# A one-core decoder layer: the step sizes' products in stacked float32r parts, the first normalisation on ScalarE, and orders planned anew

## The chip, the cores and the metric

One core of a Trainium2 chip runs one decoder layer in one launch. The metric is the device time in microseconds (us) of one execution, the median of several runs. A core has TensorE (matmuls, into PSUM), VectorE (DVE), ScalarE (ACT), GpSimd (POOL) and SyncE (SP), whose queue starts all DMAs here.

## The reference

The input x is 4 batches of 512 rows of 512. Three parts are each added to x; the layer norm before each has no gain and no bias.

```python
x = x + attn(layernorm(x), w_qkv, w_o)       # 16 heads of 32, rotary, causal softmax
x = x + ssm(ctx, z=layernorm(x), ...)        # selective scan, 16 states, 512 channels
x = x + ffn(layernorm(x), w_fc, w_proj)      # two ternary linears 512 -> 2048 -> 512, each with
                                             # its own layer norm, gelu between
# the scan's inputs, per batch (L = 512):
u = silu(conv4(in_proj_w @ ctx) + conv_b)                     # [512 channels, L]
x_dbl = x_proj_w @ u                                          # [48, L]: 16 step rows, 16 B, 16 C
delta = softplus(dt_proj_w @ x_dbl[:16] + dt_proj_b)          # the step sizes, [512, L]
state = state * exp(delta * A) + (delta * u) * B_t            # A = -exp(A_log), a recurrence over L
y = sum_n state_n * C_n + D * u;   y = y * silu(z)
```

The step-size product must keep float32 precision, since delta stands in an exponent.

## The kernel before

All activations of a batch stay in SBUF. Attention works on 32 slots (a pair of heads of one batch: `s` scores, `e` exponentials, `t` transposes, `pv` and `rz` output and row sums). The state space part has 16 states per batch; each state is two pieces of 128 partitions by two times 512 columns: ScalarE makes the factors (`exp`, L1502), GpSimd the inputs (`dbu`, L1382, with a row of B broadcast by DMA, ring of two), VectorE scans (L1911), TensorE transposes the result (`ht`, L1834), VectorE adds it times C into y (L1933). The last batch is scanned in two halves. The feed-forward part works on 16 tiles of 128 rows (`fc` L1881, `proj` L1891); it needs the tile's x after the state space part and can begin once attention is over. The ternary weights are made on the way (`wsum`, `tern`).

These parts are interleaved. The order of the work on each of the five engines is written out before the kernel by `plan()`: `follows(item)` lists for each item on which engines it runs, how long in the planner's view and what it needs; `schedule()` gives each item a due time out of tables of numbers (`WEIGHT`, `SLOT_AT`, `STATE_AT`, `FRONT`, `SSM_FRONT` and more), and `plan()` picks for each engine the ready item with the earliest due time. It also places the results in PSUM banks and sets how many filler transposes (L1708) TensorE does before an item. Each engine runs its list strictly in order, and waits on semaphores.

Around the change, per batch:

- First layer norm, 4 tiles of 128 rows, two buffers `x_in`. SP loads the tile; VectorE takes mean and variance (`ln1a`, L1940 to L1944); GpSimd takes the power -0.5 (L1435); VectorE normalises in place (`ln1b`, L1949); TensorE transposes (L1721); ScalarE copies into `xn_t` (L1543).
- Step sizes. TensorE projects u into 48 rows (`xproj`, L1739), ScalarE copies them into `x_dbl` (L1565), which frees the bank. SP stores the B rows to DRAM (L1272), from where they are broadcast. TensorE transposes the C rows (`ct`, L1748) and makes four products of [16 x 128] by [16 x 512] in float32 (`dt`, L1755). ScalarE makes four operations of each (L1583 to L1589), then VectorE (batch 0) or GpSimd (batches 1 to 3) puts `delta` together, and GpSimd multiplies by u (`du`, L1409).

`Own.done` and `Own.settle` are an engine's wait for its own earlier instructions.

Of the kernel before, what the change touches and what calls it, by code (L numbers as in the profile page):

```python
# [5 lines left out]
F32 = mybir.dt.float32  # L6
# [7 lines left out]
P = 128  # L14
# [23 lines left out]
CH = 256  # L38
HALF_L = L // 2
# [43 lines left out]
def scan_before(j):  # L83
# [25 lines left out]
WEIGHT = {'pe': {'ln1b': -40.55,  # L109
        'inproj': -66.23,  # L110
        'xproj': 52.84,
        'ct': 36.01,
        'dt': 36.18,
        'rot': -16.7,
        'v': 28.68,
        's': 10.49,
        't': 0.51,
        'pv': -14.56,
        'rz': -9.8,
        'wo': 20.24,  # L120
        'ht': -8.38,
        'gt': 52.57,
        'wtot': 64.6,
        'xt': 153.75,
        'fc': -34.46,
        'ht_ffn': 7.6,
        'proj': 117.47},
 'act': {'carry': -68.1,
         'exp': 22.09,
         'skip': -67.92,  # L130
         'ht': -65.82,
         'ln1b': 172.89,
# [36 lines left out]
         'ht_ffn': 69.64,
         'fc': -48.69,  # L170
         'hstat': 223.03,
         'hn': -111.41,
         'hq': 17.54,
         'proj': 159.09},
 'pool': {'delta': 72.43,
          'dbu': -26.46,
          'du': -36.26,
          'lo': 113.37,
          'xadd': -42.2,
          'ln1a': -84.79,  # L180
          'ln2a': 128.64,
          'xa': -39.22,
          'xc': -52.97,
          'hstat': -183.22,
          'rot': -14.91,
          'xt': 51.35,
          'ht_ffn': -79.49},
 'sp': {'xload': -185.09,
        'cload': -80.68,
        'wload': -88.67,  # L190
        'lo': -89.88,
        'xproj': -71.92,
        'bcload': 100.82,
        'stack': 114.14,
        'resid': 7.11,
        'x2store': 63.43,
        'fwload': -65.57,
        'fxload': -41.54,
        'proj': 96.57,
        'tstore': 61.26,  # L200
        'twload': -63.21,
        'xt': 86.28,
        'ht_ffn': -16.23}}

SLOT_AT = [-70.63, -1.1, -20.34, 0.54, 115.31, 113.43, 78.09, 84.3, 153.3, 152.56, 215.37, 144.34, 186.75, 225.59, 239.97,
 325.62, 293.69, 254.46, 305.8, 346.92, 332.64, 445.39, 439.93, 450.71, 470.36, 463.38, 493.97, 567.05, 578.9,
 568.09, 553.9, 607.86, 786.52]

STATE_AT = [[-17.64, -2.42, 62.4, 26.71, 61.61, 103.25, 162.05, 173.2, 146.17, 89.95, 152.03, 51.3, 193.65, 157.21, 168.06,
  150.72],  # L210
 [191.57, 187.06, 218.99, 260.04, 204.72, 261.35, 243.06, 286.61, 294.78, 379.55, 307.54, 422.57, 367.67, 396.65,
  396.57, 447.53],
 [446.31, 544.57, 382.08, 534.02, 388.94, 578.24, 382.41, 635.04, 607.17, 663.93, 751.89, 725.61, 755.13, 667.46,
  787.52, 1081.77],
 [752.3, 624.59, 697.07, 746.88, 725.98, 520.82, 754.79, 594.25, 720.37, 634.17, 682.62, 610.64, 746.41, 688.17,
  656.56, 687.14, 673.05, 780.99, 733.21, 805.86, 823.88, 779.55, 826.28, 843.2, 719.63, 839.02, 824.33, 637.9,
  921.74, 785.09, 853.63, 766.31]]
# [1982 lines left out]
```

## Time and profile before

| | |
|---|---|
| median of 3 runs | 970.09 us (966.22 to 970.52) |
| profiled execution | 970.87 us, span 969.1 us, mean granted TensorE clock 0.979 |
| TensorE busy | 893.0 us, 92%, 5426 instructions |
| VectorE busy | 854.3 us, 88%, 1167 |
| ScalarE busy | 735.0 us, 76%, 1476 |
| GpSimd busy | 615.8 us, 64%, 439 |
| DMA | 153.55 MB, mean 158 GB/s |

The span is from the first to the last instruction of the profiled execution; 1.8 us of its time lie around it. TensorE has two rows, PE for matmuls and PEld for weight loads, which overlap. A float32 matmul stands as two records; a float32r one as one record, although its type is printed as f32. Two neighbouring records overlap in time, so what an operation occupies is read from start to next start.

### The profile page before, as it was taken

The numbers are of one execution on the slowest core, as the hardware profiler recorded it, in microseconds if no ns is written. First come the engines' busy times: TensorE is split into PE (matmuls) and PEld (weight loads), VectorE is DVE, ScalarE is ACT, GpSimd is POOL, SyncE is SP. The second block draws the span as 40 slices with busy tenths as digits, with TensorE's granted clock in tenths as the row PEclk, the third lists the DMA queues.
The fourth block names the chain that finished last, engine by engine and source line by source line (L and its number), as shares of the span: only waits on it lengthen the run. The fifth ranks groups of instructions, "written<-read, shape, count | busy, mean of one in ns | idle before, by whom it ended". The sixth has DMA issues, their size and how long they took to land.

```text
span 969.1 us, 17249 instructions
## 1 busy us (share of the span) xinstructions
PE 893.0 (92%) x5426; PEld 573.7 (59%) x5426; DVE 854.3 (88%) x1167; ACT 735.0 (76%) x1476; POOL 615.8 (64%) x439
## 2 busy tenths in 40 slices
PE   7998779889999999989999999789889999999998
PEld 5464546556776656677656577567745455544544
DVE  4698999999999979899998989999989989998741
ACT  4988955935757996786988775896589999999551
POOL 0286954655347638993663989535679889878620
PEclk9999999799999999999999999799999999999999
DMA  6678849778847555274734645643147566755383
GB/s 211 234 225 267 224 124 230 197 206 216 225 144 205 165 182 148 72 210 112 185 101 136 206 132 183 220 110 111 38 72 179 112 135 129 151 106 125 62 166 77
DMA packets 146296, 153.55 MB, mean 158 GB/s; under 512 B 90448, under 2 KB 94800, under 8 KB 145952
## 3 DMA queue, kind: packets, MB, share of 16 engines
q1 hardware_dynamic: 146208, 152.45, 59.0%
q8 instruction: 46, 0.75, 0.3%
q14 instruction: 42, 0.34, 0.1%
HBM read 103.00 MB, written 28.44 MB: 136 GB/s over the span
## 4 chain that ended last, share of the span: by engine, by line
PE 45%; ACT 17%; DVE 15%; issue 11%; POOL 8%; DMA 3%; SPq 1%; ACTq 0%; POOLq 0%; DVEq 0%
PE ps L1765 7%; PE ps L1891 7%; PE ps L1834 6%; PE ps L1881 5%; DVE hb L1911 5%; ACT p_q L1615 4%; POOL hb L1382 4%; PE ps L1808 3%; ACT ps L1502 3%; PE ps L1778 3%; PE ps L1846 3%; DVE y_acc L1933 2%; ACT p_t L1631 2%; PE ps L1739 2%; DVE m_col L2008 2%
## 5 line engine op out<-in xcount | busy, mean ns | idle before, releaser
L1382 POOL TENSOR_TENSOR hb<-du,b_bc 128x1024 f32<-128x1024 f32 (+1 forms) x160 | 308.4, 1951 | 93.1 <-PE ps L1834 87.3
L1911 DVE TENSOR_TENSOR_SCAN hb<-ps,hb 128x1024 f32<-128x1024 f32 (+1 forms) x128 | 256.6, 2012 | 15.8 <-ACT ps L1502 12.2
L1502 ACT ACTIVATE ps<-delta,a_neg 128x511 f32<-128x511 f32 (+2 forms) x320 | 179.4, 598 | 86.2 <-DVE hb L1911 82.0
L1933 DVE SCALAR_TENSOR_TENSOR y_acc<-ps,ct,y_acc 128x512 f32<-128x512 f32 x256 | 178.6, 736 | 14.0 <-PE ps L1834 13.3
L1834 PE MATMUL ps<-ident,hb 128*128 128x128 f32 x1088 | 150.7, 281 | 24.8 <-DVE hb L1911 8.3
L1834 PEld LDWEIGHTS ps<-ident,hb 128*128 128x128 f32 x1088 | 124.0, 143 | 55.4 <-issue 16.5
L1615 ACT ACTIVATE p_q<-ps,m_col 128x512 f32<-128x512 f32 (+3 forms) x256 | 132.0, 538 | 10.5 <-DVE m_col L2008 9.5
L1765 PE MATMUL ps<-xn_t,w_ring 128*128 128x512 f32 x256 | 120.7, 616 | 1.0 <-ACT p_t L1631 0.5
L1881 PE MATMUL ps<-t_fc,xt 128*128 128x512 f16 x512 | 116.6, 379 | 1.8 <-ACT h_sb L1679 1.8
L1891 PE MATMUL ps<-t_pr,ht 128*128 128x512 f16 x512 | 113.0, 379 | 0.5 <-DMA ht<-hs 0.5
L1631 ACT ACTIVATE p_t<-ps 128x512 f32<-128x512 f32 x160 | 86.0, 612 | 26.8 <-PE ps L1808 26.6
L1808 PE MATMUL ps<-ident,p_q 128*128 128x128 f32 x640 | 88.0, 284 | 14.8 <-ACT p_q L1615 7.0
L1808 PEld LDWEIGHTS ps<-ident,p_q 128*128 128x128 f32 x640 | 73.0, 145 | 34.3 <-ACT p_q L1615 14.7
L2008 DVE TENSOR_REDUCE m_col<-ps 128x1 f32<-128x512 f32 (+2 forms) x192 | 86.3, 500 | 3.3 <-PE ps L1793 2.8
L1891 PEld LDWEIGHTS ps<-t_pr,ht 128*128 128x128 f16 x512 | 49.8, 98 | 60.2 <-issue 0.8
L1881 PEld LDWEIGHTS ps<-t_fc,xt 128*128 128x128 f16 x512 | 49.9, 98 | 55.0 <-ACT h_sb L1679 2.3
L1765 PEld LDWEIGHTS ps<-xn_t,w_ring 128*128 128x128 f32 x256 | 48.2, 198 | 53.7 <-issue 50.4
L1789 PE MATMUL ps<-k_st,q_st 128*128 128x512 f32 (+3 forms) x256 | 70.3, 377 | 7.8 <-DVE y_acc L1933 5.0
L1137 POOL TENSOR_TENSOR hs<-h_sb,hs 128x1024 f16<-128x1024 f32 x28 | 60.3, 2161 | 8.6 <-ACT hs L1669 8.6
L1416 POOL TENSOR_TENSOR hl<-hl 128x512 f32<-128x512 f32 x16 | 21.6, 1348 | 67.7 <-DVE hl L1996 67.7
L1778 PE MATMUL ps<-w_ring,xn_t 128*128 128x256 f32 x256 | 58.2, 381 | 2.5 <-DMA w_ring<-in_w_attn 2.2
L1846 PE MATMUL ps<-w_ring,o_t 128*128 128x256 f32 x256 | 57.4, 380 | 1.2 <-DVE xr L2031 1.0
(137 smaller groups left out, 1484.2 us busy)
## 6 DMA issues: line engine op xcount, KB each, us to landing
w_ring<-in_w_attn SPq DMA_DIRECT2D x32, 512.0 KB, 4.5
qk_d<-hl SPq DMA_DIRECT2D x64, 256.0 KB
q_st<-qk_d SPq DMA_DIRECT2D x64, 256.0 KB, 4.4
b_bc<-bc_d SPq DMA_DIRECT2D x48, 256.0 KB, 4.5
raw<-in_w_fc SPq DMA_DIRECT2D x16, 512.0 KB, 4.6
raw<-in_w_pr SPq DMA_DIRECT2D x16, 512.0 KB, 5.2
k_st<-qk_d SPq DMA_DIRECT2D x32, 256.0 KB, 4.6
k_st<-qk_d SPq DMA_DIRECT2D x64, 128.0 KB, 4.7
```

Of the source, the lines that this page charges most:

```text
L1382: nc.gpsimd.tensor_tensor(piece_of(e, hi, lo).rearrange("p (a n) -> p a n", a=2), du[b % 2][:, 2 * h:2 * h + 2, lo:hi], b_bc[:, i % BC_RIN ...
L1502: ins = nc.scalar.activation(factors(j, hi, lo)[:, (hi - lo) * m + start:(hi - lo) * (m + 1)], delta[b % 2][:, et, lo + start:hi], ACT.Exp ...
L1615: ins = nc.scalar.activation(p_q[:, h, Q_AT[i]:Q_AT[i] + w], src[:, col:col + w], ACT.Exp, bias=m_col[:, i, h:h + 1], accum_out=z_sum[:, b ...
L1631: nc.scalar.activation(dst, src, ACT.Copy).then_inc(p_ready, 1)
L1765: mm = nc.tensor.matmul(bank(kind, *a), w_ring[:, c % 2, d, P * half:P * half + P], xn_t[:, d, :], start=(d == 0), stop=(d == KD - 1))
L1808: mm = nc.tensor.transpose(dst[:, at:at + P], p_q[:, h, Q_AT[i] + P * jt:Q_AT[i] + P * jt + P], ident[:])
L1834: mm = nc.tensor.transpose(bank(kind, *a)[:, P * et:P * et + P], piece_of(2 * r + et // 2, hi, lo)[:, at:at + P], ident[:])
L1881: mm = nc.tensor.matmul(bank(kind, t, n), xt[:, t % 2, KD * m + d, :], t_fc[:, d, 512 * n:512 * n + 512], start=(d == 0 and m == 0), stop= ...
L1891: mm = nc.tensor.matmul(bank(kind, t), ht[t % 2][:, k // 8, 8 * m + k % 8, :], t_pr[:, k, :], start=(k == 0 and m == 0), stop=(k == FT - 1 ...
L1911: v.tensor_tensor_scan(h, d, h, 0.0, ALU.mult, ALU.add).then_inc(scan_done, 1)
L1933: v.scalar_tensor_tensor(out=y, in0=bank(kind, r, tb), scalar=ct[:, b % 2, tb, n:n + 1], in1=y, op0=ALU.mult, op1=ALU.add).then_inc(y_free ...
L2008: ins = v.tensor_reduce(m_col[:, i, h:h + 1], src[:, col:col + P * (i + 1)], AX.X, ALU.max, negate=True)
```

## The change

- The step rows of the projection's weights are repeated four times, and the C rows now stand before the B rows: 96 output rows (`XP`), of which 64 (`DT`) are the step rows.
- ScalarE copies the 64 step rows into `x_dt`, whose type is float32r, which rounds them to a high part; in a second instruction it copies the other 32 rows. VectorE then writes over the second half of the 64 rows the difference of the PSUM rows and the high part: the low part. The bank is freed, and the B rows' store starts, after that.
- `dt_w` is made once, by three VectorE instructions: rows 0 to 15 and 32 to 47 hold the high part of the weights, rows 16 to 31 and 48 to 63 the low part. The sum over 64 rows is then (high + low) times (high + low), in one float32r matmul for each of the 16 products.
- The normalisation of the first layer norm becomes an item `ln1n` of ScalarE: x times rstd plus nmr; GpSimd makes nmr = -mean * rstd in one more instruction.
- The planner's durations for the changed items are set, those of the score products are lowered by 0.05 (0.04 for one), and all tables of due times have other numbers, so the orders on all engines, the banks and the fillers differ.

```diff
+DT = 4 * DR
+XP = DT + 2 * DS
...
-SLOT_AT = [-70.63, -1.1, -20.34, 0.54, 115.31, 113.43, 78.09, 84.3, 153.3, 152.56, 215.37, 144.34, 186.75, 225.59, 239.97,
+SLOT_AT = [-154.69, -89.9, -187.93, -159.6, 26.3, -64.33, -131.32, 36.72, 34.04, -84.04, 17.82, 28.17, 96.66, 131.5, 255.6,
...
-EMPTIED_BY = {"ln1b": "act", "inproj": "dve", "xproj": "act", "ct": "act", "dt": "act", "v": "act", "pv": "dve",
+EMPTIED_BY = {"ln1b": "act", "inproj": "dve", "xproj": "dve", "ct": "act", "dt": "act", "v": "act", "pv": "dve",
...
-        yield "pool", 0.52, [dve(*item)]
+        yield "pool", 0.95, [dve(*item)]
+    elif kind == "ln1n":
+        yield "act", 0.62, [pool("ln1a", *a)]
     elif kind == "ln1b":
         b, t = a
-        yield "dve", 0.6, [pool("ln1a", *a)]
-        yield "pe", 0.45, [dve(*item)]
+        yield "pe", 0.45, [act("ln1n", *a)]
...
-        yield "sp", 0.3, [act(*item)]
+        yield "dve", 0.6, [act(*item)]
+        yield "sp", 0.3, [dve(*item)]
...
-        yield "pe", 1.0, [act("xproj", a[0])]
+        yield "pe", 0.36, [dve("xproj", a[0])]
...
-        yield "pe", (0.38, 0.48, 0.4, 0.38, 0.52)[n], [sp("stack", p)]
+        yield "pe", (0.33, 0.43, 0.36, 0.33, 0.47)[n], [sp("stack", p)]
...
+        x_dbl_at = base[0]
+        x_dt = sb("x_dt", [DT, L], F32R)
+        base[0] = x_dbl_at
+        x_dbl = sb("x_dbl", [XP, L])
...
+        dt_rows = rz_t[0:DT, :]
+        dt_sel = sb("dt_sel", [DT, 2])
...
-                    nc.gpsimd.tensor_tensor(rstd[:, i % 2], mv[:, i % 2, 1:2], neg_half[:, 0:1], ALU.pow)\
+                    own.done(nc.gpsimd.tensor_tensor(rstd[:, i % 2], mv[:, i % 2, 1:2], neg_half[:, 0:1], ALU.pow))
+                    own.settle()
+                    nc.gpsimd.tensor_scalar(nmr[:, i % 2], mv[:, i % 2, 0:1], rstd[:, i % 2], -1.0, ALU.mult, ALU.mult)\
                         .then_inc(ln1_rstd, 1)
...
+                elif kind == "ln1n":
+                    act.wait_ge(ln1_rstd, i + 1)
+                    nc.scalar.activation(x_in[:, i % 2, :], x_in[:, i % 2, :], ACT.Identity, bias=nmr[:, i % 2],
+                                         scale=rstd[:, i % 2]).then_inc(ln1_done, 1)
...
-                    nc.scalar.activation(x_dbl[:], bank(kind, *a)[0:DR + 2 * DS, :], ACT.Copy).then_inc(m_free["act"], 1)
+                    nc.scalar.activation(x_dt[0:DT, :], bank(kind, *a)[0:DT, :], ACT.Copy).then_inc(dt_hi, 1)
+                    nc.scalar.activation(x_dbl[DT:XP, :], bank(kind, *a)[DT:XP, :], ACT.Copy).then_inc(dt_hi, 1)
...
-                        mm = nc.tensor.matmul(bank(kind, *a)[0:DR + 2 * DS, :], xp_w[:, et, :], du[b % 2][:, et, :],
+                        mm = nc.tensor.matmul(bank(kind, *a)[0:XP, :], xp_w[:, et, :], du[b % 2][:, et, :],
...
-                    nc.tensor.matmul(bank(kind, *a), dt_w[:, P * et:P * et + P], x_dbl[0:DR, :], start=True, stop=True)\
+                    pe.wait_ge(dt_w_ready, 1)
+                    nc.tensor.matmul(bank(kind, *a), dt_w[:, P * et:P * et + P], x_dt[0:DT, :], start=True, stop=True)\
...
-                elif kind == "ln1b":
-                    dve.wait_ge(ln1_rstd, i + 1)
-                    v.tensor_scalar(x_in[:, i % 2, :], x_in[:, i % 2, :], mv[:, i % 2, 0:1], rstd[:, i % 2],
-                                    ALU.subtract, ALU.mult).then_inc(ln1_done, 1)
...
+                    if i == 0:
+                        consts(dve, "scan")
+                        own.done(v.tensor_copy(dt_w[:], dt_rows))
+                        own.settle()
+                        own.done(v.scalar_tensor_tensor(out=dt_w[:], in0=dt_rows, scalar=dt_sel[:, 0:1],
+                                                        in1=dt_w[:].bitcast(F32), op0=ALU.mult, op1=ALU.subtract))
+                        own.settle()
+                        v.tensor_scalar(dt_w[:], dt_w[:].bitcast(F32), dt_sel[:, 1:2], None, ALU.mult)\
+                            .then_inc(dt_w_ready, 1)
+                elif kind == "xproj":
+                    dve.wait_ge(dt_hi, 2 * b + 2)
+                    v.tensor_tensor(x_dt[2 * DR:DT, :], bank(kind, *a)[2 * DR:DT, :], x_dt[2 * DR:DT, :].bitcast(F32),
+                                    ALU.subtract).then_inc(m_free["dve"], 1)
```

## Rows read from the trace of the kernel before

**Rows 1.** The page, part 1: busy us of each engine, share, instructions.

```profile
PE 893.0 (92%) x5426; PEld 573.7 (59%) x5426; DVE 854.3 (88%) x1167; ACT 735.0 (76%) x1476; POOL 615.8 (64%) x439
```

**Rows 2.** Windows: stretch, length, busy PE, PEld, DVE, ACT, POOL, clock, DMA.

```profile
50.00:750.00 700.00, 639.87 (x4172) 438.44 (x4171) 656.71 (x865) 528.81 (x1164) 461.47 (x279) 0.97 0.60 167
800.00:969.00 169.00, 164.70 (x839) 83.94 (x837) 124.15 (x196) 123.04 (x170) 103.23 (x104) 1.00 0.57 117
600.00:625.00 25.00, 19.58 (x128) 15.05 (x127) 22.85 (x33) 17.59 (x36) 15.26 (x8) 0.81 0.75 263
```

**Rows 3.** The page, part 4: the chain that ended last, by engine.

```profile
PE 45%; ACT 17%; DVE 15%; issue 11%; POOL 8%; DMA 3%; SPq 1%; ACTq 0%; POOLq 0%; DVEq 0%
```

**Rows 4.** Waits: who waited for whom, total us, times, longest.

```profile
POOL hb L1382 <- PE ps L1834: 87.3, 27, 14.7
ACT ps L1502 <- DVE hb L1911: 82.0, 50, 5.1
...
DVE hb L1911 <- ACT ps L1502: 12.2, 14, 2.5
...
POOL hb L1382 <- DMA b_bc<-bc_d: 5.5, 1, 5.5
```

**Rows 5.** Timeline of TensorE (start, us, what), and the window of L1755.

```profile
538.53 1.12 PE L1755 MATMUL ps<-x_dbl,dt_w 16*128 16x512 f32 x2
539.59 0.50 PE L1789 MATMUL ps<-k_st,q_st 128*128 128x384 f32 x2
...
540.33 0.48 PE L1789 MATMUL ps<-k_st,q_st 128*128 128x512 f32 x1
540.66 0.23 PE L1793 MATMUL ps<-mask_qk,ident_b 128*128 128x128 bf16 x1
...
50.00:750.00 700.00, 13.71 (x24) 3.51 (x24) 0.97 0.60 167
```

**Rows 6.** The chain in order of time, at the start: start, us, what.

```profile
26.07 3.63 PE ps L1739 x8
...
31.21 1.45 PE ps L1755 x3
...
39.74 1.06 PE ps L1755 x2
```

**Rows 7.** Groups by form: the projection's weight loads; busy, mean ns.

```profile
L1739 PEld LDWEIGHTS ps<-du,xp_w 128*48 128x48 f32 x32 | 3.9, 133 | 14.2 <-issue 9.1 <-ACT du L1557 5.2
```

**Rows 8.** Groups by form: the copy of the projection, a PSUM product.

```profile
L1565 ACT ACTIVATE x_dbl<-ps 48x512 f32<-48x512 f32 x4 | 2.4, 592 | 5.6 <-PE ps L1739 5.6
...
L1995 DVE TENSOR_TENSOR hl<-ps,sin 128x512 f32<-128x512 f32 x16 | 10.8, 677 | 1.3 <-PE ps L1765 1.3
```

**Rows 9.** Timelines of ScalarE, SyncE and VectorE in batch 3.

```profile
536.39 0.59 ACT L1565 ACTIVATE x_dbl<-ps 48x512 f32<-48x512 f32 x1 [3.18 <-PE ps L1739]
...
541.07 1.97 SPq L1272 DMA_DIRECT2D bc_d<-x_dbl x1
...
539.47 2.28 DVE L1911 TENSOR_TENSOR_SCAN hb<-ps,hb 128x1024 f32<-128x1024 f32 x1
```

**Rows 10.** The normalisation: group, min/median/max ns, who waited, window (VectorE busy).

```profile
L1949 DVE TENSOR_SCALAR x_in<-x_in,mv,rstd 128x512 f32<-128x512 f32 x16 | 11.1, 696 | 1.2 <-POOL rstd L1435 1.2
...
L1949 DVE TENSOR_SCALAR x_in<-x_in,mv,rstd x16: 519/537/2114, 5.4 to 430.6; 128x512 f32<-128x512 f32 x16
...
  PE ps L1721: 0.7, 1
...
50.00:750.00 700.00, 8.89 (x12) 0.97 0.60 167
```

**Rows 11.** Groups by form: ScalarE with bias and scale, GpSimd on one column.

```profile
L1649 ACT ACTIVATE gate<-xr,nmr,rstd 128x512 f32<-128x512 f32 x12 | 8.8, 803 | 0.0
...
L1692 ACT ACTIVATE h_sb<-h_sb,fh 128x1024 f32<-128x1024 f32 x32 | 37.9, 1230 | 14.3 <-POOL fh L1464 14.1
...
L1464 POOL TENSOR_SCALAR fh<-fh 128x1 f32<-128x1 f32 x16 | 4.3, 267 | 1.7
```

More of the change, by code:

```diff
@@ L381 @@
-TILE = {'fxload': [67.7],
- 'xa': [-61.73],
- 'xc': [19.62],
- 'xt': [-153.78],
- 'fc': [63.84, -11.77, -60.85, 55.39],
- 'hstat': [-293.9],
- 'hn': [-257.45, -184.6],
- 'ht_ffn': [-10.09, 47.13],
- 'proj': [44.44]}
-FIRST_TILE = {'xa': [5.78], 'xc': [-2.03]}
-SWITCH = 42.4
+WEIGHT = {'pe': {'ln1b': -36.08,
+        'inproj': -45.26,
+        'xproj': 103.91,
+        'ct': 3.57,
+        'dt': 111.63,
+        'rot': 15.14,
+        'v': 90.9,
+        's': 20.17,
+        't': -10.46,
+        'pv': -93.87,
+        'rz': -28.65,
+        'wo': -3.31,
+        'ht': -2.83,
+        'gt': 79.98,
+        'wtot': 108.36,
+        'xt': 91.73,
+        'fc': -25.21,
+        'ht_ffn': -175.74,
+        'proj': 168.97},
+ 'act': {'carry': -180.28,
+         'exp': -10.78,
+         'skip': -85.43,
+         'ht': 35.19,
+         'ln1b': 167.78,
+         'inproj': -9.88,
+         'silu': 193.15,
+         'xproj': 33.71,
+         'ct': -71.76,
+         'dt': 136.96,
+         'hi': -132.84,
+         'v': -74.72,
+         'e': 308.11,
+         't': -49.41,
+         'pv': 31.22,
+         'rz': -132.91,
+         'gate': 59.92,
+         'xt': -156.09,
+         'ht_ffn': 22.89,
+         'fc': -44.96,
+         'wsum': -26.9,
+         'hn': -153.58,
+         'ln1n': 44.92},
+ 'dve': {'scan': -6.81,
+         'ht': 11.64,
+         'ln1a': 205.42,
+         'ln1b': 118.45,
+         'inproj': 30.16,
+         'delta': -122.02,
+         'rot': -13.44,
+         's': -35.28,
+         'rz': 52.41,
+         'pv': -118.61,
+         'wo': -61.51,
+         'ln2a': 58.47,
+         'ln2b': 105.95,
+         'gt': 8.05,
+         'wtot': 10.35,
+         'tern': -153.27,
+         'xa': 209.96,
+         'xc': 29.97,
+         'xt': 172.73,
+         'ht_ffn': -3.38,
+         'fc': -108.86,
+         'hstat': 85.41,
+         'hn': -76.46,
+         'hq': -36.6,
+         'proj': 126.61,
+         'xproj': -50.8},
+ 'pool': {'delta': 48.95,
+          'dbu': -109.83,
+          'du': 12.42,
+          'lo': 231.3,
+          'xadd': 16.32,
+          'ln1a': -177.38,
+          'ln2a': 116.29,
+          'xa': -59.88,
+          'xc': 57.4,
+          'hstat': -172.59,
+          'rot': 51.6,
+          'xt': 31.11,
+          'ht_ffn': 87.44},
+ 'sp': {'xload': -125.39,
+        'cload': 46.16,
+        'wload': 221.75,
+        'lo': -153.22,
+        'xproj': -136.62,
+        'bcload': 140.56,
+        'stack': 176.33,
+        'resid': 89.77,
+        'x2store': 185.22,
+        'fwload': 1.49,
+        'fxload': 113.95,
+        'proj': -7.88,
+        'tstore': -150.71,
+        'twload': -54.25,
+        'xt': 284.74,
+        'ht_ffn': 46.19}}
@@ L395 @@
+TILE = {'fxload': [385.29],
+ 'xa': [57.64],
+ 'xc': [-78.83],
+ 'xt': [-84.77],
+ 'fc': [162.32, -77.58, 53.2, 129.02],
+ 'hstat': [-91.7],
+ 'hn': [-415.04, -251.35],
+ 'ht_ffn': [30.71, 120.66],
+ 'proj': [286.74]}
+FIRST_TILE = {'xa': [-417.34], 'xc': [-440.81]}
+SWITCH = 73.52
 PATIENCE = 0.18
@@ L1745, in _ @@
                     emptied(pe, TASK["xproj", b])
[L1746 removed]
+                    rows = slice(DT, DT + DS)
                     for tb in range(LT):
@@ L2148, in constants @@
         "ident": np.eye(P, dtype=np.float32),
+        "dt_sel": np.tile(np.repeat(np.array([[0, -1], [1, 1]], np.float32), DR, axis=0), (2, 1)),
     }
```

431 lines of the change are left out of this document (170 added, 261 removed), and 12 rows, old and new, of tables (ATTN_END, SKIP).

## The prediction

> **What bounds the kernel now.** I read the page's busy row first, then the same by stretch. TensorE is busy 893.0 of 969.1 us and VectorE 854.3; ScalarE has 735.0 and GpSimd 615.8 [rows 1]. By stretch [rows 2] the two leaders change places. From 50 to 750 us (attention and state space together) VectorE is busy 656.7 of 700 us, TensorE 639.9, ScalarE 528.8, GpSimd 461.5. From 800 us to the end TensorE is at 164.7 of 169 with VectorE at 124.2: the feed-forward products alone set the end there. The chain of waits [rows 3] says the same: 45% of it is TensorE, 17% ScalarE, 15% VectorE. The waits show who hurries whom [rows 4]: ScalarE waited 82.0 us for VectorE's scans, VectorE only 12.2 us for ScalarE's factors, so ScalarE is the one with room. Work saved after 50 us moves the end one for one only if it stands on the engine that bounds at that moment: VectorE mostly, TensorE next to it.
>
> **Step 1, the step-size products.** There are 16, each two records on TensorE. Two records start at 538.53 and the next product at 539.59: 1.06 us for one product of 512 columns [rows 5]. The change makes each one pass in float32r with 64 rows instead of 16. The score products (k_st, q_st) already are float32r with 512 columns: one starts at 540.33, its mask product at 540.66, so 0.33 us [rows 5]. That row is the same kind of operation, so I take 0.33; its own duration of 0.48 us is the upper end (none can be dearer than 1.06, a gain is sure). Gain 0.73 each, 11.7 us of TensorE for 16; 12 of them lie in 50 to 750 us (24 records), 8.8 us. The four at the start come below.
> The Trainium skill, FP8 and Floating Point Precision (TensorE Precision Notes), says true float32 takes four passes through the array. By that rule alone a product would be a quarter of 1.06, 0.27 us, and the 16 would give 12.6 us instead of 11.7; the row shows that the float32r product costs more than the quarter, and I keep the row.
>
> **Step 2, the same product's stationary side.** The projection before it (xproj) now has 96 output rows for 48. Its moving side is unchanged, so its groups of 3.6 us [rows 6], one per batch, stay. Its 32 weight loads take 3.9 us together [rows 7] and lie under the matmuls before them; twice the columns cost 0, at worst another 3.9 us.
>
> **Step 3, splitting high and low.** Per batch ScalarE copies twice (64 and 32 partitions) where it copied once at 0.59 us [rows 8]; VectorE gains a subtraction out of PSUM, 0.68 us by the like instruction with one PSUM and one SBUF input [rows 8]; 4 batches: 2.4 us ScalarE, 2.7 us VectorE. The products, and the store of the B rows, now wait for VectorE. Queued behind the subtraction on VectorE are scans and y sums; queued behind the products on TensorE are scores and y transposes. In batch 3 the old copy ended at 536.98, the first product ran at 538.53, and the store was issued only at 541.07 because SyncE was busy with others [rows 5, 9]: 1.5 us and 4 us of cover. A subtraction that meets a scan waits up to 2.28 us [rows 9]. With 0.5 us for the second copy that is 0.5 + 2.28 + 0.68 = 3.5 us at worst and 1.2 at best, so mostly covered in batches 1 to 3; price taken 0 beyond the busy time, kept as a rival. Once, VectorE also makes the signed weights: a copy and a tensor_scalar like the old normalisation, 0.54 us each [rows 10], and a combination of two inputs, 0.68 [rows 8]: 1.8 us.
>
> **Step 4, the normalisation.** VectorE loses 16 instructions, 11.1 us; 12 of them, 8.9 us, after 50 us [rows 10]. Their median is 0.537 us but the longest 2.11, so 16 medians would be 8.6: 2.5 us are stalls, and they go too. The Trainium skill, SBUF — State Buffer (Who interferes with whom), says such a float32 tensor_scalar from SBUF to SBUF can lock the port pair that VectorE shares with GpSimd, and that ScalarE waits for no one. By that rule the stall is not passed to ScalarE, the trace agrees in the spread 0.519 to 2.114, and without the stalls the gain would be 8.6 and not 11.1.
> ScalarE gains 16 of 128x512 with bias and scale. With both operands it does 512 elements (Silu) in 0.80 us and 1024 in 1.23, half of which is 0.62 [rows 11]; I take 0.70 between them: 11.2 us, ends 9.8 and 12.9. GpSimd gains 16 products of one column, 0.27 us by its like, and a settle of about 0.1: 6 us [rows 11]; it idles 238 us in the middle. The path of one tile grows by 0.27 + 0.1 + (0.70 - 0.54), 0.5 us. TensorE waited 0.7 us in all for the old instruction [rows 10]: cover is there in batches 1 to 3, 0 us. What ScalarE's greater load costs: in the middle it gains 8.4 + 1.8 = 10.2 us on 171 us of idle time, 6%; VectorE's waits for its factors are 12.2 us [rows 4], 6% of that is 0.7 us. Below nothing it cannot be; above, all 10.2.
>
> **Step 5, the start.** Here VectorE idles and the chain is latency: convolutions, projection at 26.07, copy, products, softplus [rows 6]. The weight making sits behind the first convolution, whose successors are queued on VectorE: 1.8 us late. Then 0.5 for the second copy and 0.68 for the subtraction: +3.0. Of the chain 1.45 + 1.06 = 2.5 us are old products, which shrink to a third: -1.7. Net +1.3 (0 to 3). The larger constants (64 rows for 16, 96 columns for 48) land long before 26 us.
>
> **Step 6, all orders anew.** Every engine's order and the PSUM bank choice come from a planner with new numbers, and no row of before shows the result. Nothing excludes a sign. Bound: VectorE idles 43 us in the middle [rows 2]; a quarter regained or as much lost is 11 us either way. I take 0 and leave it in the range.
>
> **The sum.** In the middle VectorE saves 8.9 - 3 x 0.68 = 6.9 us, TensorE 8.8 us. If VectorE alone bounds, 6.9 count; if the two bound in turn at different moments, both count, 15.7. I take the middle, 11.3, since the busy shares are 94% and 91% and the last 169 us are TensorE's alone, which takes whatever is finished earlier. By the chain's shares alone it would be less: 11.7 x 0.45 + 8.4 x 0.15 - 13.6 x 0.17 - 6 x 0.08 = 3.7 us; that is the low end. Total -11.3 + 1.3 + 0.7 = -9.3. The profiled execution took 970.9 us (span 969.1 and 1.8 around it), which gives 961.6; it lies 0.8 above the median of 970.1, so 961.
>
> **Rivals.** About 0.5%, 4.9 us, is what a measurement can tell from no change: under 965.2 is faster, over 974.9 slower.
> *Both savings count and the orders fill gaps too*: 970.1 - 15.7 + 2.0 is 956, and part of the 11 us of step 6 brings it to 950 (945 to 956). For: VectorE and TensorE are both short of full in the middle. Against: GpSimd waited 87.3 us for y transposes [rows 4], so the ring buffers and not the engines' lengths set part of the pace.
> *The gain is eaten in the middle*: 970 (966 to 975). Mechanism: TensorE with less to do is granted a lower clock. In 600 to 625 us it was busy 19.6 of 25 us and was granted 0.81, the mean of 1.2 and 2.4 GHz with 38% of the time at the lower [rows 2]; that is 4.8 us of full-speed work lost. Two more such stretches, or ScalarE's 10.2 us in full, cancel 9 us. Against: products of 0.73 us are scattered, and that stretch is starved by its neighbours. The Trainium skill, TensorE: Matmul & The Clock Gate (HAM oscillation), says the same, that gaps on the array bring the clock down; the trace agrees with 0.81 there and 1.00 where TensorE is dense.
> *Slower*: the subtraction on VectorE. Per batch the products and the B rows come 3.5 us later; if the scans of a batch start that much later, 4 x 3.5 = 14 us, 961 + 14 = 975, and with part of step 6 lost 977. It decides once the lateness passes the 1.5 us of cover seen in batch 3. For: batch 3 has one GpSimd wait of 5.5 us for a B row [rows 4]. Against: in batch 3 the scans of batch 2 still run, so VectorE has other work.
> *The product isn't one pass*: TensorE saves nothing, VectorE's 6.9 remain: 970.1 - 6.9 + 2.0 + 1.7 (the start's saving, gone) = 967, inside the second rival.
>
> **How the numbers follow.** Forecast case 0.44 (956 to 966), both in full 0.20, eaten 0.18 (one pass failing included), slower 0.18. Faster by over 0.5%: 0.40 of the first case and 0.20, 0.60. Within: 0.04 and 0.18, 0.22. Slower: 0.18. For 8 in 10 the range takes in most of both outer cases: 946 to 978; the likeliest case's own is 956 to 966.
>
> **What would show it.** The products in one record each with a next start after 0.3 to 0.4 us; TensorE's busy time near 881; VectorE's near 848 and no normalisation on it; ScalarE's near 749; the first scan no more than 2 us later than before; VectorE over 94% busy in the middle. The forecast is wrong if the middle is not shorter by about 9 us, if VectorE's waits for ScalarE's factors exceed 25 us, or if the granted clock falls below 0.97 of full.

## The result

The changed kernel took 977.14 us (976.35 to 978.44, four runs) beside 969.54 us for the kernel before on the same chip: 1.0086 times as long, 95% interval 1.0059 to 1.0113, so 0.6 to 1.1% slower. The forecast was 961 us, a gain; the time came out 16 us above it, on the other side of the kernel before. It lies inside the stated range only because the slower rival reached there.

The profiled execution took 977.26 us (span 975.4). The page, parts 1 and 4:

```profile
PE 895.6 (92%) x5439; PEld 584.7 (60%) x5439; DVE 847.1 (87%) x1158; ACT 753.2 (77%) x1498; POOL 618.4 (63%) x455
...
PE 56%; ACT 16%; DVE 12%; issue 12%; POOL 2%; DMA 1%; SPq 0%; ACTq 0%; DVEq 0%; POOLq 0%
```

Beside [rows 1]: VectorE lost 7.2 us, as forecast (847.1; forecast 848). TensorE lost nothing: 895.6, forecast 881. And the span grew by 6.3 us. A lighter VectorE did not end earlier: its last scans of the state space part begin at 902.61 us before and at 912.99 us now.

```profile
902.61 1.38 DVE L1919 TENSOR_TENSOR_SCAN hb<-ps,small,hb 128x256 f32<-128x256 f32 x2
...
912.99 2.66 DVE L1947 TENSOR_TENSOR_SCAN hb<-ps,small,hb 128x256 f32<-128x256 f32 x4
```

They end at 903.99 and 915.65, 11.7 us apart; what is behind them became 5.4 us shorter. The groups by form of the changed operations:

```profile
L1783 PE MATMUL ps<-x_dt,dt_w 64*128 64x512 f32 x16 | 7.7, 490 | 0.0
...
L1766 PE MATMUL ps<-du,xp_w 128*96 128x512 f32 x32 | 16.4, 660 | 4.1 <-ACT du L1583 4.1
...
L1561 ACT ACTIVATE x_in<-x_in,nmr,rstd 128x512 f32<-128x512 f32 x16 | 12.8, 807 | 3.9 <-POOL nmr L1455 3.8
...
L1455 POOL TENSOR_SCALAR nmr<-mv,rstd 128x1 f32<-128x1 f32 x16 | 4.3, 270 | 1.6
...
L2002 DVE TENSOR_TENSOR x_dt<-ps,x_dt 32x512 fp32r<-32x512 f32 x4 | 2.7, 684 | 5.9 <-ACT x_dbl L1592 5.9
...
L1591 ACT ACTIVATE x_dt<-ps 64x512 fp32r<-64x512 f32 x4 | 2.4, 592 | 3.7 <-PE ps L1766 3.7
L1592 ACT ACTIVATE x_dbl<-ps 32x512 f32<-32x512 f32 x4 | 2.4, 588 | 0.1
```

Each operation has nearly its forecast length. A product is now one record of 0.49 us; all of them take 7.7 us for 17.9 before, so 10.2 us of TensorE's busy time went. The normalisation on ScalarE takes 0.807 us, the upper end of what was allowed, and GpSimd's extra column 0.27. None of these lengths explains a loss. The same windows as [rows 2], with one at the start (columns as there; clock after POOL):

```profile
25.00:50.00 25.00, 22.93 (x83) 13.70 (x83) 13.54 (x26) 21.90 (x38) 6.19 (x9) 0.93 0.60 198
50.00:750.00 700.00, 637.43 (x4146) 443.84 (x4146) 643.55 (x843) 536.48 (x1167) 457.00 (x284) 0.96 0.59 166
600.00:625.00 25.00, 21.44 (x150) 16.32 (x148) 24.66 (x35) 17.28 (x26) 19.31 (x11) 0.99 0.62 231
800.00:969.00 169.00, 164.84 (x847) 85.95 (x845) 131.75 (x205) 131.78 (x189) 109.30 (x109) 0.99 0.56 114
```

VectorE is less full in the middle, 643.55 for 656.71 of the same 700 us. TensorE's matmuls there take only 2.4 us less, where the products alone account for 7.3 (6.45 us now for 13.71 [rows 5]): there are more fillers, and the clock fell to 0.96 from 0.97. Over the whole span of the two profiles the mean clock fell from 0.979 to 0.970. With levels of 2.4 and 1.2 GHz that is 2 x 0.030 x 975 = 58 us at the lower one, for 2 x 0.021 x 969 = 41. The waits, who waited for whom (us in total, times, longest):

```profile
POOL hb L1400 <- PE ps L1862: 111.7, 32, 13.4
...
ACT ps L1522 <- DVE hb L1939: 68.4, 39, 5.2
...
DVE st_h L2156 <- ACT h_sb L1706: 21.6, 13, 7.4
...
ACT p_q L1642 <- DVE m_col L2044: 15.4, 7, 6.4
DVE hb L1939 <- ACT ps L1522: 14.2, 19, 2.1
```

Beside [rows 4], GpSimd waits 24 us longer for TensorE's y transposes, and VectorE only 2 us longer for ScalarE's factors (14.2, far from the 25 set as a bound), while ScalarE waits 14 us less for the scans. No single one of these waits holds the loss.

At the start, the window of 25 to 50 us of the kernel before is to be set beside the one above:

```profile
25.00:50.00 25.00, 23.93 (x86) 13.09 (x87) 16.48 (x28) 22.28 (x38) 8.19 (x7) 1.00 0.62 214
```

TensorE and VectorE are to be read together there. TensorE's timeline (start, us, what, idle before it in brackets):

```profile
27.07 5.37 PE L1766 MATMUL ps<-du,xp_w 128*96 128x512 f32 x8 [4.08 <-ACT du L1583]
...
34.55 0.73 PE L1783 MATMUL ps<-x_dt,dt_w 64*128 64x512 f32 x2
...
39.10 7.07 PE L1806 MATMUL ps<-w_ring,xn_t 128*128 128x256 f32 x32
46.10 0.50 PE L1783 MATMUL ps<-x_dt,dt_w 64*128 64x512 f32 x1
46.53 3.70 PE L1793 MATMUL ps<-xn_t,w_ring 128*128 128x512 f32 x8
50.16 0.49 PE L1783 MATMUL ps<-x_dt,dt_w 64*128 64x512 f32 x1
```

VectorE's timeline:

```profile
15.74 2.32 DVE L1987 SCALAR_TENSOR_TENSOR du<-ps,small,du 128x511 f32<-128x511 f32 x3 [8.57 <-ACT du L1578]
17.98 0.41 DVE L1992 CAST dt_w<-rz_t 64x512 fp32r<-64x512 f32 x1
18.42 0.74 DVE L1994 SCALAR_TENSOR_TENSOR dt_w<-rz_t,dt_sel,dt_w 64x512 fp32r<-64x512 f32 x1
19.20 0.48 DVE L1997 TENSOR_SCALAR dt_w<-dt_w,dt_sel 64x512 fp32r<-64x512 f32 x1
19.61 6.75 DVE L1987 SCALAR_TENSOR_TENSOR du<-ps,small,du 128x511 f32<-128x511 f32 x9
...
33.72 0.68 DVE L2002 TENSOR_TENSOR x_dt<-ps,x_dt 32x512 fp32r<-32x512 f32 x1 [5.33 <-ACT x_dbl L1592]
...
59.29 2.28 DVE L1939 TENSOR_TENSOR_SCAN hb<-ps,hb 128x1024 f32<-128x1024 f32 x1
```

The three instructions on the weights hold the convolutions up from 17.98 to 19.61. Two products stand together at 34.55, and the next matmul starts at 35.22: 0.34 us for each. Behind a single one it starts 0.42 to 0.43 us later (46.10 to 46.53, 50.16 to 50.58), for 1.05 us before. The projection took 5.37 us for 3.63 before [rows 6], at a lower clock (0.93 from 25 to 50 us, for 1.00 before). The new orders put 32 records of v (L1806) ahead of the third product, where 16 stood; it starts at 46.10 for 39.74 [rows 6], and the fourth at 50.16. The first scan came at 59.29; in the trace of before it starts at 53.04.

### The profile page after: what moved, and what is told of

Read it like the earlier page. It is cut to its first block, busy times and chain, and to the rows that moved or that the text cites. A ratio compares the mean times of both kernels' runs of the same rounds, so it can differ in the third digit from the quotient of the medians.

```text
span 975.4 us, 17297 instructions
## 1 busy us (share of the span) xinstructions
PE 895.6 (92%) x5439; PEld 584.7 (60%) x5439; DVE 847.1 (87%) x1158; ACT 753.2 (77%) x1498; POOL 618.4 (63%) x455
## 4 chain that ended last, share of the span: by engine, by line
PE 56%; ACT 16%; DVE 12%; issue 12%; POOL 2%; DMA 1%; SPq 0%; ACTq 0%; DVEq 0%; POOLq 0%
PE ps L1793 9%; PE ps L1862 8%; PE ps L1919 6%; PE ps L1806 5%; PE ps L1909 5%; PE ps L1836 5%; PE ps L1874 4%; ACT ps L1522 3%; DVE hb L1939 3%; ACT p_q L1642 3%; PE ps L1848 2%; PE ps L1757 2%; DVE y_acc L1961 2%; DVE m_col L2044 2%; PE ps L1817 2%
## 5 line engine op out<-in xcount | busy, mean ns | idle before, releaser
L1939 DVE TENSOR_TENSOR_SCAN hb<-ps,hb 128x1024 f32<-128x1024 f32 (+1 forms) x128 | 257.2, 2014 | 17.1 <-ACT ps L1522 14.2
L1862 PE MATMUL ps<-ident,hb 128*128 128x128 f32 x1088 | 146.8, 280 | 19.7 <-DVE hb L1939 6.6
L1836 PE MATMUL ps<-ident,p_q 128*128 128x128 f32 x640 | 92.9, 294 | 17.2 <-ACT p_q L1642 12.0
L1836 PEld LDWEIGHTS ps<-ident,p_q 128*128 128x128 f32 x640 | 77.5, 151 | 34.8 <-ACT p_q L1642 19.5
L1817 PE MATMUL ps<-k_st,q_st 128*128 128x512 f32 (+3 forms) x256 | 75.3, 387 | 10.7 <-ACT p_q L1642 4.8
L2156 DVE BATCH_NORM_STATS2 st_h<-h_sb 128x6 f32<-128x512 f32 x64 | 41.2, 681 | 21.8 <-ACT h_sb L1706 21.6
L1806 PE MATMUL ps<-w_ring,xn_t 128*128 128x256 f32 x256 | 58.1, 382 | 0.1
```

Source lines behind the costliest of these rows:

```text
L1806: mm = nc.tensor.matmul(bank(kind, *a)[:, CH * m:CH * m + CH], xn_t[:, d, P * t:P * t + P], w_ring[:, wc % 2, d, :], start=(d == 0), stop= ...
L1836: mm = nc.tensor.transpose(dst[:, at:at + P], p_q[:, h, Q_AT[i] + P * jt:Q_AT[i] + P * jt + P], ident[:])
L1862: mm = nc.tensor.transpose(bank(kind, *a)[:, P * et:P * et + P], piece_of(2 * r + et // 2, hi, lo)[:, at:at + P], ident[:])
L1939: v.tensor_tensor_scan(h, d, h, 0.0, ALU.mult, ALU.add).then_inc(scan_done, 1)
```

## The experiments

Each was timed in five rounds beside the kernel before on the same chip. Ratios are to it; percentages turned into us use 969.5. Differences of two experiments are worked from their ratios, their intervals from the two half widths added in squares. In e1 to e3 and all built on them, the orders, banks and fillers are those of the kernel before, and only the changed items are put in or taken out.

**The edits apart, orders fixed.** Two theories stood: the new orders lose the time, or the edits do.

```diff
 e1: both edits; e2: only the float32r products; e3: only the normalisation
+EMPTIED_BY["xproj"] = "dve"
+for b in range(B):
+    insert("dve", ("xproj", b), STARTS["act", ("xproj", b)] + 0.5)
+for item in [x for x in ORDER["dve"] if x[0] == "ln1b"]:
+    ORDER["dve"].remove(item)
+    insert("act", ("ln1n", *item[1:]), STARTS["dve", item])
 e4: the changed kernel's orders, the operations of before
+for item in [x for x in ORDER["act"] if x[0] == "ln1n"]:
+    ORDER["act"].remove(item)
+    insert("dve", ("ln1b", *item[1:]), STARTS["act", item])
+ORDER["dve"] = [x for x in ORDER["dve"] if x[0] != "xproj"]
+EMPTIED_BY["xproj"] = "act"
```

> Both edits (stacked float32r step-size products, normalisation on ScalarE), but the orders, PSUM banks and fillers of the kernel before: the new items are only inserted into its lists (ln1n on ScalarE where VectorE had its normalisation, the low-part subtraction on VectorE after ScalarE's copy). Theory S (the start: weights made between the convolutions, the split's latency and a cold TensorE cost some 3 us, the new orders of the start another 3, and later savings are lost in waits): 965 to 972, first scan near 56 us instead of 59.3. Rival O (the new orders as a whole are the cause and the edits themselves give what was forecast): about 961. Rival M (the edits themselves cost): 975 to 979, like the changed kernel.

> Only the stacked float32r products, in the orders of the kernel before. Theory S: the later products save 8 us of TensorE, the start loses 3; 966 to 970. Rival O: 963. Rival M with the split as the culprit: 973 or more.

> Only the normalisation on ScalarE, in the orders of the kernel before. VectorE loses 11.1 us, ScalarE gains 16 x 0.80 = 12.8. Theory S and rival O: VectorE bounds the middle, 963 to 967. Rival M with ScalarE as the culprit: 970 or more, with VectorE's waits for ScalarE's factors above 14 us.

> Neither edit, but the orders, banks and fillers of the changed kernel (its normalisation put back on VectorE at ScalarE's place, the subtraction left out). Rival O: the orders are the cause, 975 to 985 (they were made for shorter products, so a bit worse than the changed kernel). Theory S: the orders cost only their start, 972 to 977. Rival M: the orders are harmless, 969 to 971.

| | us | ratio |
|---|---|---|
| changed kernel | 977.14 | 1.0086 (1.0059 to 1.0113) |
| e1 both edits, old orders | 978.57 | 1.0080 (1.0051 to 1.0109) |
| e2 products alone | 976.95 | 1.0071 (1.0049 to 1.0094) |
| e3 normalisation alone | 971.31 | 1.0013 (0.9995 to 1.0031) |
| e4 old operations, new orders | 991.10 | 1.0221 (1.0198 to 1.0244) |

The edits alone cost what the change costs: e1 and the changed kernel differ by 0.6 +- 3.8 us. They add up: 6.9 for the products and 1.3 for the normalisation, 8.2 in sum, 7.8 in e1. With both edits in, the new orders neither cause nor cure the loss. But they are not neutral: with the old operations they cost 21.4 us. So "orders 0" held for the pair and not for the orders. Read the other way round, the same two numbers say that under the new orders the two edits together save 13.1 +- 3.4 us (e4 less the changed kernel), while under the old orders they cost 7.8. In both comparisons the orders were made for the operations of only one side, and the items of the other were put in by hand. What an edit is worth depends on the orders; everything that follows, except e5 and e7, is told of the old ones.

**Inside the float32r edit.** Three theories stood: the late weights at the start cost the time, or the subtraction and its wait do, or TensorE's own saving is given back by the clock. e10 is e2 with the three weight instructions right behind `a_neg`, where VectorE idles for 8.6 us; e15 is e10 without the subtraction; e12 is e2 with the 64-row product in float32; e11 is the kernel before with a float32r product of 16 rows, without low parts.

```diff
 e10, e5:  dve.tensor_scalar(a_neg, ...)
+          consts(dve, "scan"); the three dt_w instructions
 ...
-          if i == 0: consts(dve, "scan"); the three dt_w instructions
 e15:      EMPTIED_BY["xproj"] = "act"; no item on VectorE; rows 32 to 63 as ScalarE wrote them
 e12:      matmul(dt_w.bitcast(F32), x_dt.bitcast(F32))
 e11:      x_dt = sb([DR + 2 * DS, L], F32R); dt_w rounded by one tensor_copy
```

> As e2_dt_old (976.95), but VectorE makes the split weights before its first convolution, where it idles from 7 to 16 us, and not after it. In e2 the making delayed the projection, TensorE idled before it and ran it at the lower clock. Theory S (the start is a fixed delay that nothing later absorbs): the first scan comes 2 to 3 us earlier and the time falls by as much, 973 to 975. Rival W (the start's delay is absorbed by slack, the cost is VectorE's subtraction and the clock in the middle): 976 to 977.

> As e10_dt_old_early (973.32) without VectorE's subtraction: the bank is freed and products and B rows go after ScalarE's second copy (left out: the low part of the activations; all 64 rows are high parts). Theory V (what is left of the edit's cost is VectorE's work and the wait behind its scans): 969.5 to 971. Rival: it is the second copy and the wider projection, 972.5 to 974.

> As e2_dt_old with copies, subtraction, weights and waits, but the product of the 64 stacked rows in float32, four passes as before. Against e2 it differs by one pass alone. Theory T: 976 to 980, at most 3 us above e2. Rival F: 985 or more, e2's 976.95 plus the 8.8 us of the middle.

> The kernel before with its 16 step-size products as one float32r pass of 16 rows, without low parts (left out: the low parts of both operands, and B and C are rounded too). No second copy, no subtraction, no wider projection; only TensorE's saving of 16 x 0.7 us remains. Theory T (TensorE's saving is worth nothing in the middle because VectorE and the waits set the pace there): 967 to 970. Rival F (the forecast's account, TensorE's saving counts): 959 to 962.

| | us | ratio |
|---|---|---|
| e10 early weights | 973.32 | 1.0038 (1.0018 to 1.0057) |
| e15 and no subtraction | 970.66 | 1.0017 (1.0006 to 1.0028) |
| e12 float32 products | 977.67 | 1.0078 (1.0054 to 1.0101) |
| e11 one pass alone | 970.30 | 1.0005 (0.9988 to 1.0021) |

The 6.9 us of e2 split into 3.2 +- 2.9 for the weights' place, 2.0 +- 2.2 for the subtraction, and 1.6 +- 1.1 for what is left in e15 (second copy, 96 columns, and the float32r product with them). The one pass is worth 0.7 +- 3.2 us (e12 less e2), or -0.5 +- 1.6 (e11): nothing that can be seen, where some 10 us of TensorE's busy time went; by e11's interval a gain of more than 1.1 us is excluded for it alone. The first batch's projection in TensorE's timeline of e2:

```profile
26.73 5.37 PE L1768 MATMUL ps<-du,xp_w 128*96 128x512 f32 x8 [4.08 <-ACT du L1585]
```

In e10:

```profile
24.21 5.37 PE L1768 MATMUL ps<-du,xp_w 128*96 128x512 f32 x8 [2.64 <-ACT du L1585]
```

In e15:

```profile
25.38 3.67 PE L1765 MATMUL ps<-du,xp_w 128*96 128x512 f32 x8 [2.63 <-ACT du L1582]
```

In e2 the projection starts 2.5 us later than in e10, and the first scan at 56.37 for 54.02, 2.4 us. Not all of this is the edit, since the first convolution, which stands ahead of e2's weights, was itself 1.1 us later. In e2:

```profile
15.40 2.32 DVE L1995 SCALAR_TENSOR_TENSOR du<-ps,small,du 128x511 f32<-128x511 f32 x3 [8.16 <-ACT du L1580]
```

In e10:

```profile
14.32 8.99 DVE L2003 SCALAR_TENSOR_TENSOR du<-ps,small,du 128x511 f32<-128x511 f32 x12 [1.18 <-ACT du L1580]
```

From there to the projection it is 11.33 us in e2 and 9.89 in e10 (9.88 in the kernel before): 1.4 us for the weights' place. Counted from the first convolution, the first scan is 4.1 us later than before in e2, 2.9 in e10 and 0.4 in e15. The 96 columns are not what makes the projection 5.37: e15 has them too and takes 3.67. It is the clock, 0.50 against 1.00 in the window of 26 to 28 us, in e10:

```profile
26.00:28.00 2.00, 2.00 (x4) 0.73 (x3) 0.55 (x1) 0.56 (x2) 0.20 (x1) 0.50 0.77 254
```

And in e15:

```profile
26.00:28.00 2.00, 2.00 (x6) 0.71 (x5) 1.45 (x5) 1.74 (x4) 0.91 (x2) 1.00 0.99 401
```

The idle time ahead of the projection does not settle the clock alone, since 2.64 us of it stand before it in e10 and 2.63 in e15. The Trainium skill, TensorE: Matmul & The Clock Gate (HAM oscillation), says that gaps on the array bring the clock down; the trace agrees for the 4.08 us here, and shows that a gap of 2.6 us can end either way.

e5 makes the same edit in the changed kernel:

> The changed kernel (977.14) with the split weights made before the first convolution, where VectorE idles, as in e10 (which gained 3.6 us over e2 in the old orders). Theory S: the projection starts 1.6 us earlier and at the full clock, first scan at 56 instead of 59.3, 973 to 974. Rival W: the new orders have slack for it behind the start, 976 to 977.

It took 973.39 us, 1.0047 (1.0032 to 1.0063): 3.8 +- 3.0 us less than the changed kernel. From the first convolution to the projection it is 9.89 us for 11.33, and the projection took 3.67 us at the full clock for 5.37. The two pairs have the same sign and size; together they give 3.5 +- 2.1. That the weights' place costs time is shown; how much of it is the 1.4 us of delay and how much follows from that is not.

**The normalisation.** Three questions: what VectorE's relief gives alone (e13), what ScalarE's work takes when TensorE doesn't wait for it (e16), and what the one pass adds once VectorE is relieved (e17).

```diff
 e13: the kernel before, normalisation left out
-     v.tensor_scalar(x_in, x_in, mv, rstd, subtract, mult).then_inc(ln1_done, 1)
+     TensorE's transpose waits for ln1_rstd
 e16: e3, but
-     nc.scalar.activation(x_in[:, i % 2, :], x_in[:, i % 2, :], ACT.Identity, bias, scale)
+     nc.scalar.activation(aside, x_in[:, i % 2, :], ACT.Identity, bias, scale)
+     TensorE's transpose waits for ln1_rstd; SyncE's next load of the buffer also for ScalarE
 e17: e13 and e11 together
```

> The kernel before with the first layer norm's normalisation left out (x goes to the transposes as it was loaded); VectorE loses 11.1 us, ScalarE and GpSimd gain nothing. Forecast's account: the 8.9 us of the middle count, 961. Theory T extended (single savings inside fixed orders vanish in waits on the other engines): 966 to 970. If it is 961, then e3_norm_old (971.3) lost the gain to ScalarE's 12.8 us.

> As e3_norm_old (normalisation on ScalarE at the same place), but its result goes to a bfloat16 tile that nobody reads, and TensorE transposes x as loaded (left out: the normalisation). ScalarE and GpSimd have their work, VectorE's is gone, and TensorE no longer waits for ScalarE. Theory A (ScalarE's 12.8 us of work eat the gain of e13): 970 to 972, as e3. Rival L (the wait of TensorE for ScalarE's instruction eats it): 965 to 967, as e13.

> e13 and e11 together: no normalisation and step-size products in one pass of 16 rows (left out: the normalisation and the low parts). Forecast's middle account (both savings count when the engines bound in turn): 4 us or more below e13's 964.9, at most 961. Rival V (TensorE's saving is worth nothing even with VectorE relieved by 11 us): 964 to 966.

| | us | ratio |
|---|---|---|
| e13 no normalisation | 964.87 | 0.9951 (0.9932 to 0.9971) |
| e16 aside | 968.91 | 0.9998 (0.9979 to 1.0018) |
| e3 as changed | 971.31 | 1.0013 (0.9995 to 1.0031) |
| e17 none, and one pass | 968.47 | 0.9993 (0.9976 to 1.0010) |

Taking 11.1 us off VectorE, with nothing put anywhere, gives 4.8 +- 1.9 us. The work put on ScalarE and GpSimd takes 4.6 +- 2.7 of it back, although TensorE doesn't wait for ScalarE in e16; it still waits for GpSimd's extra column, and the next load of the buffer for ScalarE. Which of the two engines' work costs it was not separated. TensorE's wait for ScalarE adds 1.5 +- 2.6, not established. Adding the one pass to the relieved kernel makes it slower by 4.1 +- 2.5 us, though TensorE has less to do. The windows of 375 to 400 and 400 to 425 us, where two of batch 2's four products run, show one place where something changes. Before:

```profile
375.00:400.00 25.00, 22.41 (x178) 16.67 (x177) 21.94 (x25) 20.61 (x47) 23.51 (x13) 1.00 0.56 159
400.00:425.00 25.00, 22.94 (x127) 16.59 (x126) 24.04 (x28) 17.54 (x36) 24.52 (x16) 1.00 0.45 129
```

e11, one pass alone:

```profile
375.00:400.00 25.00, 22.58 (x171) 16.75 (x170) 21.69 (x24) 19.30 (x45) 22.83 (x13) 0.93 0.55 156
400.00:425.00 25.00, 21.74 (x117) 16.15 (x116) 23.44 (x27) 16.53 (x32) 24.52 (x16) 0.93 0.44 129
```

e13, no normalisation:

```profile
375.00:400.00 25.00, 23.62 (x182) 16.44 (x181) 23.71 (x29) 19.74 (x46) 24.49 (x14) 1.00 0.49 146
400.00:425.00 25.00, 22.40 (x134) 17.28 (x132) 24.38 (x34) 20.11 (x48) 24.09 (x16) 1.00 0.72 181
```

e17, both:

```profile
375.00:400.00 25.00, 22.47 (x170) 16.12 (x169) 20.66 (x24) 19.01 (x44) 22.78 (x13) 0.93 0.56 160
400.00:425.00 25.00, 21.77 (x118) 17.04 (x117) 23.49 (x30) 17.51 (x36) 24.61 (x14) 0.93 0.46 135
```

Read the number behind GpSimd's in each (the clock) with the count of TensorE's records. With the shorter products the clock is 0.93 in both windows, without them 1.00, and in e11 the matmuls of 375 to 400 us are fewer (171 for 178) but no shorter in sum (22.58 for 22.41). Two windows of 25 us at 0.93 are 3.5 us of full-speed work lost, of some 7.6 us that the shorter products save in the middle. Each is one profile, but there are twelve with the old orders. In the six with float32 products (before, e3, e8, e12, e13, e16) both windows have 1.00; in the six with float32r ones at least one has less: e1 0.93 in the first, e2 0.96 in the second, e10 0.86 and 0.99, e15 0.86 in the first, e11 and e17 0.93 in both. In the changed kernel, whose orders are others, both have 1.00, and its 58 us at the lower level lie elsewhere. So the place is shown for the old orders only.

That the clock eats the whole saving is not shown. Over all timed runs the mean clock is clearly lower with the one pass in one pair of three: e17 0.974 for 0.980 in e13, which is 6 us of full-speed work. In e11 it is 0.976 for 0.977, and in e2 0.971 for 0.972 in e12, both within the spread of the runs, and there the saving is just as invisible.

**More fillers.** If the lower clock were the cause and fillers its cure, more of them should help.

```diff
+FILLS = {item: int(1.6 * n) for item, n in FILLS.items()}
```

> The changed kernel with 1.6 times as many filler transposes in each place where it has some. Theory C (what the one-pass products save is given back because TensorE idles more and its clock is lowered more often: 58 us at the lower level in the changed kernel's profile, 41 before): fewer stretches at 1.2 GHz, mean clock 0.975 or more, 973 to 975. Rival N (the clock is a symptom, fillers only delay what waits): 977 to 981.

> The kernel before with 1.6 times as many fillers in each place. Theory C: a smaller gain than in the changed kernel, 966 to 969. Rival N: 970 to 974.

The changed kernel with them took 980.15 us, 1.0110 (1.0092 to 1.0128); the kernel before 972.48, 1.0032 (1.0018 to 1.0046). TensorE's busy time rose by 10.1 and 9.5 us. The page's part 1 of the changed kernel with more fillers:

```profile
PE 905.7 (93%) x5559; PEld 595.8 (61%) x5559; DVE 847.3 (87%) x1158; ACT 752.4 (77%) x1498; POOL 620.0 (64%) x455
```

And of the kernel before with more fillers:

```profile
PE 902.5 (93%) x5529; PEld 585.0 (60%) x5529; DVE 855.2 (88%) x1167; ACT 735.6 (76%) x1476; POOL 615.3 (63%) x439
```

The mean clock of the profiles stayed: 0.972 for 0.970 and 0.979 for 0.979. Over all runs it is 0.969 for 0.971 in the changed kernel and 0.980 for 0.978 in the kernel before. Of the places, those with one filler kept one; there are 120 and 103 more records in all. The changed kernel is 2.3 +- 3.1 us slower with them, the kernel before 3.1 +- 1.4. Fillers in these places are only in the way. Since they raised the clock by 0.002 at most, they don't test what a higher clock would be worth.

## Why the prediction was wrong, step by step

- **Step 1, the products.** One pass, as said, but somewhat longer: 0.34 us to the next start for the two that stand together, 0.42 to 0.43 for most, 0.33 taken. The score product with its mask product behind it was the shortest case and not the like one. The gain is 0.63 us for most, 10.2 us of busy time for 11.7. TensorE's busy time did not fall by that all the same: fillers grew by 3.6 us (28.7 to 32.3), the attention's transposes (p_q) from 88.0 to 92.9.
- **Step 2, wider projection.** A group takes 3.60 to 3.67 us at the full clock, as the 3.63 before, so its weight loads are hidden, as said. With the second copy it is part of the 1.6 +- 1.1 us of e15, for 0.
- **Step 3, the subtraction.** Priced at 0 in the batches, it measured 2.0 +- 2.2, not told from 0; it has the sign of the slower rival and a seventh of its 14 us. The cover seen in batch 3 was real: from the projection's start to the first product it is 5.8 us before (532.72 to 538.53) and 5.8 in e10 (537.66 to 543.41). The first batch has none: 4.6 us before (26.07 to 30.68), 7.8 in e10 (24.21 to 32.01), of which 1.7 are the slower projection.
- **Step 4, the normalisation.** The busy times came out (0.81 for 0.70 on ScalarE). The price did not: 4.8 gained and 4.6 to 6.1 given back, where 8.9 and 0.7 stood. Pricing ScalarE's 10.2 us by its share of VectorE's waits (6%) was wrong: that wait is 9.4 us in the profiles of e13 and e16 alike, and the time went up all the same. ScalarE feeds TensorE and GpSimd too; through which of them, or through GpSimd's own extra work, the loss comes is open.
- **Step 5, the start.** The term +1.3 (0 to 3) was too small. The first scan came 3.3 us later in e2 and 6.3 in the changed kernel, counted from the first convolution 4.1 and 6.7; the new orders add the rest. Two things were left out: the projection took 1.7 us more at a lower clock, and the orders moved the last two products. The weights' place measured 3.5 +- 2.1 for the 1.8 taken, an interval that holds 1.8. The lower clock does not make the difference in both pairs, since e10's projection has it too.
- **Step 6, orders.** 0 held for the change as a whole (0.6 +- 3.8), by luck: the orders cost 21.4 us with the old operations, and the two edits save 13.1 +- 3.4 under the new orders and cost 7.8 under the old.
- **The sum is the step that failed.** It took 6.9 to 15.7 us of saving in the middle as real, halfway between "VectorE bounds" and "both bound in turn". Measured in the old orders: TensorE's saving (8.8 us there by the forecast, 7.6 by the trace) is worth 0, VectorE's 8.9 to 11.1 are worth 4.8, and the work on ScalarE and GpSimd, priced at 0.7, takes 4.6. So neither engine, at 94% and 91%, passed on what it saved. The low end that the chain's shares gave, 3.7, was nearer only by luck: its terms were 5.3 for TensorE (0 measured), 1.3 for VectorE (4.8) and 2.8 for ScalarE and GpSimd (4.6). The rival of the eaten gain was nearest for the middle. Its mechanism, the lower clock, is seen in two windows; that it is the cause is not shown.

With the measured terms: -4.8 (VectorE) + 4.6 (ScalarE's and GpSimd's work) + 1.5 (TensorE's wait) + 3.2 (weights) + 2.0 (subtraction) + 1.6 (second copy, width) + 0 (one pass) + 0.6 (orders) = +8.7, beside +8.3 +- 2.6 measured for the change. That the sum closes is little evidence, since most terms are neighbouring differences of one row of kernels, all with the old orders; three of them (TensorE's wait, the subtraction, the orders) are smaller than their own uncertainty.

Of the forecast's signs: VectorE near 848, one record per product and, within 4 us, ScalarE near 749 (753) were right; TensorE near 881, the first scan within 2 us and VectorE over 94% in the middle (643.55 of 700, 92%) were not. Of the three things that were to show it wrong, one came plainly: the middle was not shorter. The clock stood at 0.970, just where the bound was (0.969 to 0.974 in the four runs), and the wait for the factors stayed far below its bound.

**What stays open.** Why TensorE's saving is worth nothing in the old orders. The clock is one candidate, seen in e17's runs and in two windows, and waits of the other engines in orders made for longer products are another; nothing here held the clock fixed while the products became shorter. What each edit is worth alone under the new orders was not measured, nor which part of the new orders costs the 21.4 us. Whether orders planned for e5's operations would gain was not tried. No version ran faster than the kernel before with the whole computation in it.

## What to carry to other kernels

Time an edit with the old orders frozen before planning anew; then try the new orders with the old operations as well. Here the two comparisons differ by 21 us, so neither alone is the price of the edits or of the orders. Where engines at over 90% wait for each other, neither the busy share nor the share of the chain told what a saving was worth: TensorE had 45% of the chain and its 10 us gave nothing, VectorE had 15% and its 11.1 us gave 4.8. Leave the operation out and time that, which takes one run. Before adding even 1.6 us to a start that is all latency, look for an idle stretch of the engine ahead of it: here 8.6 us lay free one instruction earlier on VectorE.

## What the runs showed of the hardware

- Behind a 64-row float32r product of 512 columns the next matmul starts after 0.34 us (the two that stand together) or 0.42 to 0.43 us (most of the others), behind a float32 one of 16 rows (before) or 64 rows (e12) after 1.05 to 1.06: a factor of 2.5 to 3.1. The Trainium skill, FP8 and Floating Point Precision (TensorE Precision Notes), says float32 takes four passes; the trace shows two records and a factor below four, so the rule in time would promise more than there is.
- The stacked product in float32 costs no more than the 16-row one: 0.55 us a record (17.7 us for 32) in e12, 13.71 us for 24 before [rows 5]. Between 16 and 64, rows of the contraction are free here.
- ScalarE's Identity with a bias and a scale column took 0.807 us for 128x512, as its gate operation did before (0.803) [rows 11], and not half of the 1.23 us for 1024 columns. The Trainium skill, ScalarE: Activation LUTs (What ACT_TABLE_LOAD costs), gives 186 ns, 0.833 ns for each column and 93 ns for each operand that is a column; the estimate by it for 512 columns with two such operands is 0.80 us. The trace agrees, and the rule would have given the price that the forecast missed.
- Runs of one kernel differ with the clock: in e3 a run at 0.984 took 967.3 us, at 0.977 970.2, at 0.972 974.8. From first to last that is 7.5 us for 0.012 of 970, 12 us of full-speed work: about 0.6 us of time per us of work lost. Over its twelve runs the correlation of time and clock is -0.89; over the four series of the kernel before, of 17 to 24 runs, it is weaker, -0.38 to -0.62. Which comes first, the lost clock or the longer waits, these runs don't say.
